# A selective scan in a fused kernel: chunk 0's work goes first on every engine, and the rest of the layer norm waits until inside the scan

## What is computed

```python
x = x + 0.5 * _L0_ffn_ref(_layernorm(x, axis=-1), ...)   # 64 experts, top 3
x = x + _L0_attn_ref(_layernorm(x, axis=-1), ...)        # selective scan
x = x + 0.5 * _L0_ffn_ref(_layernorm(x, axis=-1), ...)   # the experts again
```

```python
raw, gate = jnp.split(x @ W_in, 2, axis=-1)
h = jax.nn.silu(conv4(raw) + conv_b)
ts, Bmat, C = jnp.split(h @ W_x, [DTR, DTR + DST], axis=-1)
dt = jax.nn.softplus(ts @ W_dt + b_dt)
dA = jnp.exp(dt[..., None] * A)                          # 256 channels x 16 states
dBu = dt[..., None] * Bmat[:, :, None, :] * h[..., None]
y = _ssm(dA, dBu, C) + h * D                             # state = dA*state + dBu; y = <state, C>
return (y * jax.nn.silu(gate)) @ W_out
```

## Time and profile before

| | |
|---|---|
| three runs | 796.94, 797.6, 801.3 us; median 797.6 us |
| the profiled execution | 802.77 us, of which its span 801.0 us |
| busy in the span | PE 667.8 us (83%), DVE 596.5 (74%), POOL 489.8 (61%), ACT 445.5 (56%) |
| granted TensorE clock, mean | 0.934 of full |
| the first expert layer | until about 221 us, with its sums from 185.66 us |
| the scan | first scan at 232.97 us, last one ends at about 589.6 us |
| the second expert layer | from about 597 us to the end |

### The profile page before, as it was taken

How to read it: one execution, slowest core, us unless ns; L and a number is a source line. 1 busy time by engine, 2 the same in 40 slices (tenths; PEclk the granted TensorE clock), 3 DMA queues, 4 the chain that set the end, 5 groups by cost and what they waited for, 6 DMA issues and landing times. The chain is left out here.

```text
span 801.0 us, 27792 instructions
## 1 busy us (share of the span) xinstructions
PE 667.8 (83%) x11782; PEld 399.5 (50%) x11782; DVE 596.5 (74%) x1014; ACT 445.5 (56%) x925; POOL 489.8 (61%) x308
## 2 busy tenths in 40 slices
PE   7537999997957989899999989888988179998957
PEld 3524555566734445454544545454546045554547
DVE  7983444443799999999999999989998944344425
...
GB/s 279 393 321 219 333 322 286 245 56 319 75 140 108 110 108 53 127 96 136 107 123 122 70 135 54 126 108 56 4 37 402 194 19 321 325 323 246 114 122 313
DMA packets 87109, 141.07 MB, mean 176 GB/s; under 512 B 9491, under 2 KB 34717, under 8 KB 85712
## 3 DMA queue, kind: packets, MB, share of 16 engines
...
...
## 5 line engine op out<-in xcount | busy, mean ns | idle before, releaser
L1380 POOL TENSOR_TENSOR BIG<-BIG,R 128x1024 f32<-128x1024 f32 x127 | 305.4, 2435 | 13.6 <-DVE BIG L1301 12.3
L1301 DVE TENSOR_TENSOR_SCAN BIG<-BIG,ps 128x1024 f32<-128x1024 f32 x128 | 285.5, 2269 | 13.5 <-PE ps L925 10.2
L925 PE MATMUL ps<-BIG,stack 64*32 64x128 f32 x8192 | 154.1, 278 | 33.2 <-DVE BIG L1301 28.7
L925 PEld LDWEIGHTS ps<-BIG,stack 64*32 64x32 f32 x8192 | 117.4, 107 | 110.9 <-DVE BIG L1301 80.8
L767 POOL DMA_INDIRECT R<-xn_dram,tok_idx x64 | 65.1, 1018 | 89.7 <-DVE row_idx L700 70.7
L781 POOL DMA_INDIRECT y_dram<-BIG,row_idx x64 | 64.6, 1010 | 84.4 <-DVE BIG L724 38.8
L1170 ACT ACTIVATE BIG<-R,An 128x510 f32<-128x510 f32 x128 | 84.3, 710 | 7.1 <-DVE BIG L1301 7.0
L724 DVE COPY BIG<-ps 128x128 f32<-128x128 f32 x64 | 18.4, 288 | 89.3 <-remote 56.8
L1170 ACT ACTIVATE BIG<-BIG,An 128x510 f32<-128x510 f32 x128 | 83.7, 708 | 0.2
L415 ACT ACTIVATE BIG<-BIG 128x512 f32<-128x512 f32 x64 | 40.2, 628 | 74.4 <-DVE BIG L716 58.1
L409 ACT ACTIVATE BIG<-ps 128x128 f32<-128x128 f32 x64 | 16.9, 265 | 111.5 <-PE ps L533 74.7
...
## 6 DMA issues: line engine op xcount, KB each, us to landing
...
```

What stands on the lines that cost most here:

```text
L925: last = nc.tensor.matmul(ps[CW * slot:CW * slot + CW, 2 * (st % 2) + b, :] .rearrange("p (g k s) -> p k g s", g=2, k=4)[:, k], dT[q % 2][ ...
L1301: nc.vector.tensor_tensor_scan(state[st % 3], dA[:, st % 6].rearrange("p b g t -> p (b g t)"), ps[:, u:u + 2, :].rearrange("p b n -> p (b ...
L1380: nc.gpsimd.tensor_tensor(prod[st % RP], state[st % 3].rearrange("p (b g t) -> p b g t", b=2, g=2), Cf[q % 2][:, 2 * gp:2 * gp + 2].rearra ...
```

## The change

Nothing of the arithmetic's amount in the scan changes; work and waits change places, and the inverse root is computed another way.

- Layer norm: the last 12 tiles' statistics move from ahead of scan 0 to behind scans 9, 10 and 12 of chunk 0. `inverse_root` (13 instructions for 24 tiles) becomes one instruction to open, a logarithm and an exponential on ACT, and four to close (`log_root_closed`), once for 12 tiles ahead of scan 0 and once for the other 12, opened behind scan 13 and closed in chunk 1 behind its scan 3.
- Buffers: `state`, `prod` and `dB` get other columns of BIG, and the decays other slots (`DECAY_SLOT`), so that waits for all eight groups of sums become waits for four, six or none.
- PE: `dbu(0)` goes ahead of `dt_proj(1, ...)`, and `dtu_transposes(0, 1)` ahead of `x_proj(1)`. `gates(0, ...)` and `dtu_transposes(1, 0)` go from behind `dbu(3)` to behind `dbu(4)`.
- ACT: `normalise(1)` goes behind the two `raw_copy(0, ...)`, the two `dtu_copy(0, ...)` ahead of `silu_of(1)`, `decays(0)` ahead of `x_parts(1)`, `decays(2)` ahead of `softplus_rest(1, 1)`, and `gate_copy(0, ...)` from behind `decays(5)` to behind `decays(6)`.
- DVE: two taps of chunk 1 go between `dt(0, 0)` and `dt(0, 1)`; `dt(1, n)` goes one scan later. POOL: `dtu(1, ...)` goes two steps later, and `diagonal(0, 3)` no longer waits for the sums.

```diff
@@ -93,3 +93,3 @@
 STAT_TOTALS = dict(stats=NI, meanvar=NI, rstd=6, root=1)
-NEWTON = 13
+DECAY_SLOT = (0, 4, 1, 5, 2, 3)
 LN_TOTALS = dict(normed=24, normed_act=8, transposed=8, xT=8)
@@ -210,5 +210,6 @@
         dA = BIG[:, 0:6144].rearrange("p (u b g t) -> p u b g t", u=6, b=2, g=2)
-        state = [BIG[:, 6144 + 1024 * u:7168 + 1024 * u] for u in range(3)]
-        prod = [BIG[:, 9216 + 1024 * u:10240 + 1024 * u].rearrange("p (b g t) -> p b g t", b=2, g=2) for u in range(RP)]
-        dB = [BIG[:, 16384 + 4096 * u:20480 + 4096 * u].rearrange("p (k n s) -> p k n s", k=4, n=NS) for u in range(2)]
+        state = [BIG[:, c:c + 1024] for c in (8192, 6144, 7168)]
+        prod = [BIG[:, c:c + 1024].rearrange("p (b g t) -> p b g t", b=2, g=2)
+                for c in (9216, 10240, 11264, 16384, 17408, 18432, 19456)]
+        dB = [BIG[:, c:c + 4096].rearrange("p (k n s) -> p k n s", k=4, n=NS) for c in (12288, 20480)]
         HH = [BIG[:, 24576 + 1024 * u:25600 + 1024 * u].rearrange("p (h t) -> p h t", h=C2) for u in range(3)]
@@ -240,20 +241,26 @@
 
-        def inverse_root(e, S, i0, i1, n):
...
-            step(nc.vector.tensor_scalar(v, mv[:, i0:i1, 1], EPS, None, ALU.add))
-            step(nc.vector.tensor_single_scalar(z.bitcast(I32), v.bitcast(I32), 1, ALU.arith_shift_right))
-            step(nc.vector.tensor_scalar(r.bitcast(I32), z.bitcast(I32), -1.0, float(0x5F3759DF), ALU.mult, ALU.add))
-            for k in range(3):
...
+        def log_root_opened(S, i0, i1):
+            nc.vector.tensor_scalar(rs[:, 0, i0:i1], mv[:, i0:i1, 1], EPS, None, ALU.add).then_inc(S("rstd"), 1)
+        def log_root_scalar(e, S, i0, i1, n, m):
+
+            e.wait_ge(*S.at("rstd", n + 1))
+            nc.scalar.activation(rs[:, 2, i0:i1], rs[:, 0, i0:i1], ACT.Ln).then_inc(S("root"), 1)
+            e.wait_ge(*S.at("root", m + 1))
+            nc.scalar.activation(rs[:, 2, i0:i1], rs[:, 2, i0:i1], ACT.Exp, scale=-0.5).then_inc(S("root"), 1)
+
+        def log_root_closed(e, S, i0, i1, n, m):
...
+            e.wait_ge(*S.at("root", m + 2))
+            nc.vector.tensor_tensor(y, z, z, ALU.mult).then_inc(S("rstd"), 1)
...
@@ -807,4 +814,4 @@
                     wait(e, "prod", STEPS * (b - 1))
-                    if b == 0:
-                        e.wait_ge(*F[0].at("sum", 8))
+                    if b < 2:
+                        e.wait_ge(*F[0].at("sum", 4 + 4 * b))
                     for slot in range(SLOTS):
@@ -913,4 +920,4 @@
                 wait(e, "scanned", st - 1)
-                if st == 0:
-                    e.wait_ge(*F[0].at("x", 8))
+                if st < 2:
+                    e.wait_ge(*F[0].at("x", 6 + 2 * st))
                 if n == 0:
@@ -999,9 +1006,9 @@
             gate_sums(e, F[0], 0, 7)
-            x_proj(1)
             dtu_transposes(0, 1)
+            x_proj(1)
+            dbu(0)
             dt_proj(1, 0)
             dt_proj(1, 1)
-            b_transposes(1)
-            dbu(0)
             dbu(1)
+            b_transposes(1)
             for q in range(NQ + 1):
@@ -1019,7 +1026,8 @@
                             sum_states(q - 1, 1, 1, 1)
-                        if q == 0:
-                            gates(0, 0)
-                            gates(0, 1)
-                        if back:
+                        if q and back:
                             dtu_transposes(b, 0)
+                    if n == 2 and q == 0:
+                        gates(0, 0)
+                        gates(0, 1)
+                        dtu_transposes(1, 0)
                     if n == 2 and front:
@@ -1071,4 +1079,3 @@
                 wait(e, "t_psum", q)
-                if q < 3:
-                    wait(e, "rstd", (6, 12, 12 + NEWTON)[q])
+                wait(e, "rstd", (6, 12, 17, 17, 17, 22, 22, 22)[q])
                 for j in range(4):
@@ -1164,8 +1171,6 @@
                 wait(e, "scanned", st - 5)
-                if st == 0:
-                    e.wait_ge(*F[0].at("sum", 8))
-                    e.wait_ge(*F[0].at("x", 8))
-                    wait(e, "pads", 4)
+                if st < 6:
+                    wait(e, "pads", 5 + 2 * (st // 2))
                 for g in range(2):
-                    last = nc.scalar.activation(dA[:, st % 6, :, g, 1:SEQ], dtR[h][:, j, :].rearrange("p (b t) -> p b t", b=2)[:, :, 1:SEQ], ACT.Exp,
+                    last = nc.scalar.activation(dA[:, DECAY_SLOT[st % 6], :, g, 1:SEQ], dtR[h][:, j, :].rearrange("p (b t) -> p b t", b=2)[:, :, 1:SEQ], ACT.Exp,
                                                 scale=An4[:, cg, 2 * gp + g:2 * gp + g + 1])
@@ -1179,5 +1184,5 @@
             xt_copy(0)
-            normalise(1)
             raw_copy(0, 0)
             raw_copy(0, 1)
+            normalise(1)
             xt_copy(1)
@@ -1191,13 +1196,14 @@
             raw_copy(1, 1)
-            silu_of(1)
-            nc.scalar.preload_act_table_set("natural_log_exp_and_others")
+            log_root_scalar(e, MST, 8, 20, 12, 2)
             dtu_copy(0, 0)
-            x_parts(1)
             dtu_copy(0, 1)
+            silu_of(1)
+            nc.scalar.preload_act_table_set("natural_log_exp_and_others")
             decays(0)
+            x_parts(1)
             decays(1)
             softplus_rest(1, 0)
+            decays(2)
             softplus_rest(1, 1)
             bt_copy(1)
-            decays(2)
             decays(3)
@@ -1210,3 +1216,3 @@
                         decays(STEPS * q + n + 4)
-                    if q == 0 and n == 1:
+                    if q == 0 and n == 2:
                         gate_copy(0, 0)
@@ -1232,2 +1238,4 @@
                         silus(q, f, run, front)
+                    if q == 0 and n == 14:
+                        log_root_scalar(e, MST, 20, NI, 17, 4)
                     if n == 11 and front:
@@ -1257,5 +1265,6 @@
 
-            def statistics(i0, i1, n):
-                wait(e, "meanvar", i1)
-                inverse_root(e, MST, i0, i1, n)
+            def first_steps(*slots):
+                for u in slots:
+                    nc.vector.memset(dA[:, u, :, :, 0:1].rearrange("p b g t -> p (b g) t"), 0.0)\
+                        .then_inc(M("pads"), 1)
 
@@ -1300,3 +1309,3 @@
                 u = 2 * (st % 2)
-                nc.vector.tensor_tensor_scan(state[st % 3], dA[:, st % 6].rearrange("p b g t -> p (b g t)"),
+                nc.vector.tensor_tensor_scan(state[st % 3], dA[:, DECAY_SLOT[st % 6]].rearrange("p b g t -> p (b g t)"),
                                              ps[:, u:u + 2, :].rearrange("p b n -> p (b n)"), 0.0, ALU.mult, ALU.add)\
@@ -1322,2 +1331,3 @@
             root_vector(e, MST, 4, 8, 6, 1)
+            first_steps(*DECAY_SLOT[0:2])
             moe_sum(e, F[0], 2)
@@ -1326,7 +1336,12 @@
             moe_sum(e, F[0], 3)
+            first_steps(*DECAY_SLOT[2:4])
             moe_sum(e, F[0], 4)
             stats(8, 20)
+            wait(e, "meanvar", 20)
+            log_root_opened(MST, 8, 20)
             dt(0, 0)
+            for m in range(2):
+                tap(1, m // 3, m % 3)
             dt(0, 1)
-            for m in range(6):
+            for m in range(2, 6):
                 tap(1, m // 3, m % 3)
@@ -1334,9 +1349,7 @@
                 moe_sum(e, F[0], g)
-            e.wait_ge(*F[0].at("x", 8))
-            nc.vector.memset(dA[:, :, :, :, 0:1].rearrange("p u b g t -> p (u b g) t"), 0.0).then_inc(M("pads"), 1)
+            first_steps(*DECAY_SLOT[4:6])
             diagonal(0, 0)
             diagonal(0, 1)
-            stats(20, NI)
-            statistics(8, NI, 12)
-            wait(e, "pads", 4)
+            log_root_closed(e, MST, 8, 20, 12, 2)
+            wait(e, "pads", 9)
             for q in range(NQ + 1):
@@ -1347,4 +1360,12 @@
                         scan(STEPS * q + n)
-                    if q == 0 and n < C2:
-                        dt(1, n)
+                    if q == 0 and n in (1, 2):
+                        dt(1, n - 1)
+                    if q == 0 and n in (9, 10, 12):
+                        i0 = 20 + 4 * (9, 10, 12).index(n)
+                        stats(i0, i0 + 4)
+                    if q == 0 and n == 13:
+                        wait(e, "meanvar", NI)
+                        log_root_opened(MST, 20, NI)
+                    if q == 1 and n == 3:
+                        log_root_closed(e, MST, 20, NI, 17, 4)
                     if q >= 1 and n == 0 and back:
@@ -1400,7 +1421,7 @@
                 for n in range(STEPS):
-                    if n < C2 and q + 1 >= 0 and q + 1 < NQ:
-                        dtu(q + 1, n)
+                    n0 = 2 if q == 0 else 0
+                    if n0 <= n < n0 + C2 and 0 <= q + 1 < NQ:
+                        dtu(q + 1, n - n0)
                     if n == 9 and q + 1 >= 0 and q + 1 < NQ:
                         if q == -1:
-                            e.wait_ge(*F[0].at("sum", 8))
                             diagonal(0, 3)
```

29 lines of the change are left out of this document (14 added, 15 removed).

## The result

The changed kernel takes 807.92 us in the median of four runs (803.87 to 809.6). The kernel before, run beside it, takes 797.63 (796.94 to 801.3). The ratio is 1.0102, with a 95% interval of 1.0057 to 1.0146: slower by 1.0%. The median lies beyond the range on record, whose upper end was 803.5.

What follows compares the result with a forecast made beforehand. It took DVE's scans to bound the kernel, with ACT and PE deciding scan 0. +0.7 us at full clock plus 2.0 for PE's lower clock gave +2.7 on the median of 797.6: 800.3 us, range 794.5 to 803.5.

Steps and rivals of the forecast that it cites:

- In chunk 1 DVE closes the root for 0.8 us: Chunk 1, ahead of where DVE waits for PE: closing the root costs 0.8 us, with nothing to hide it.
- the sum: Whole kernel: +0.7 us with PE at full clock plus 2.0 for the lower clock, +2.7 us.
- the way in: Up to scan 0: DVE ready 7.7 us earlier, but ACT and PE decide; scan 0 at 227.5, 5.5 us earlier.
- forecast for full clock: Chunks 0 and 1, PE at full clock: lead 5.5 us at scan 0, 0.1 at scan 16; cost +0.7 us.
- the clock: Chunk 0: after 4.6 us idle PE runs at 1.2 GHz from `dtu_transposes(1, 0)` to raw(2, 0), losing 2.0 us.
- (b): PE's clock low from 224 on and for 6 us from 244.1: +5.1 us, 802.7; chance 0.22.
- (a): Chunk 0's lead of 4.9 us at scan 4 survives: chance 0.15 for -4 and beyond, 0.15 for -1 to -4.
- my own case: The change does what it says at scan 0 and nothing more than the sum: -1 to +4 us, chance 0.45.
- (c): ACT's table loads each add a drain of about 1.38 us: +5.5 us, 803.1; chance 0.03.

Runs made afterwards that it cites:

- r1: The changed kernel run again unaltered, on another chip: 791.17 us, ratio 1.0107 to the kernel before.
- r3: The changed kernel with idle matmuls on PE, twelve ahead of `x_proj(1)` and nineteen ahead of `dtu_transposes(1, 0)`: 791.52 us, ratio 1.0122 to the kernel before.
- r12: The changed kernel with the same idle matmuls on PE ahead of `x_proj(1)` and `dtu_transposes(1, 0)`, run once more: 812.74 us, ratio 1.0156 to the kernel before.
- r9: The changed kernel with the root's second closing on POOL, between its products of chunk 1's fourth and fifth steps: 802.66 us, ratio 1.0031 to the kernel before.
- r6: The kernel before plus four unused small DVE instructions, one SBUF input and a constant, behind scan 3 of chunks 1 to 7: 833.15 us, ratio 1.0368.
- r2: The changed kernel with the last 12 statistics and their root's opening and closing back ahead of scan 0: 783.76 us, ratio 1.0011 to the kernel before.

## Why the prediction was wrong

**The step that failed** is "In chunk 1 DVE closes the root for 0.8 us". Its four instructions were put at 0.2 us each, from rows in which POOL ran nothing. Beside POOL's products the pauses of 0.92 and 2.28 us come, and from scan 19 to scan 20 it is 3.6 us longer than before, in every profile with small instructions at this place. What follows was not in the prediction at all: PE waits 3.19 us for the late scan, in r1, r3 and r12 its clock falls behind that, and the scans lose another 1.1 to 1.3 us. In all chunk 1 is 3.7 us (result) to 5.1 us (r12: 50.5 for 45.4) longer. r9 takes away that closing alone and chunk 1 is 45.6. The pauses alone carry the sum from +2.7 to +5.5, which is 803.1 and still just inside the range; with r12's 5.1 it is +7.0.

The rows for it stood there. The earlier trace rows has the diagonals at 2.27 and 2.92 us beside POOL. The 1.23 of the earlier trace rows, taken as the duration when POOL makes no diagonal, isn't one with POOL idle: POOL was at its products then, and it was one of them that waited. POOL's timeline before:

```profile
240.70 8.00 POOL L1380 TENSOR_TENSOR BIG<-BIG,R 128x1024 f32<-128x1024 f32 x3
```

Three products take 8.00 us where they take 7.01 elsewhere. So either of the two can be the one that waits. The prediction allowed for POOL with the large instructions and not with the small ones.

The Trainium skill ("SBUF — State Buffer", section "Who interferes with whom") states the rule that I should have weighed: VectorE with two SBUF inputs, or in a mode that uses both ports, and GpSimd take a shared pair of ports for a whole instruction, and the second blocks fully until the first is done. The trace agrees, with DVE's 2.28 us ending 0.03 us behind the end of the product. It also fits r6, since the Trainium skill ("VectorE: DVE Perf Modes", section "Mode 2×_2P — use both read ports for one tensor") counts a float32 `tensor_scalar` from SBUF among the instructions that use both.

**Right: the way in.** DVE is ready 3.7 us behind the eighth sum (forecast 4.2), ACT and PE decide scan 0, and the gate copies end at 248.25, 23.4 behind it (forecast 23.0). DVE's wait ahead of scan 5 was 2.56 us (forecast about 2; the profile names no releaser, but `dbu(5)` ended just ahead of it). With the clock kept, r3 and r12 meet the forecast for full clock at each step: scan 0 at 6.7 (6.4), scan 1 at 10.4 (10.3), scan 4 at 19.7 (19.4), scan 5 at 25.3 (25.3), scan 7 at 32.0 (32.2), scan 16 at 58.8 (59.3).

**Too small: the clock.** I put it at 2.0 us. Against r3 and r12 the changed kernel loses 1.3 to 1.4 us at scan 0, 2.3 at scan 5, 3.2 to 4.3 at scan 16, and 2.9 to 3.0 at scan 32. The part ahead of scan 0, which I had left to rival (b), did come. From the gate copies to scan 5 it was 4.1 us instead of 2.3, as the PE rows at 248.40 show.

**The sum, as measured up to scan 32:** -0.6 at scan 16 with full clock (58.8 for 59.4; forecast -0.1), +2.9 for the clock (2.0), +5.1 for the closing (0.8; in the 5.1, which is r12's, the lower clock behind the closing has some 1.1): +7.4, which is 112.2 against 104.8. The forecast was 2.7. The timed ratios of 1.0102 and 1.0107 are 8.1 and 8.4 us. From scan 32 to scan 127 the changed kernel takes 259.8 us and the one before 261.4, so nothing more was lost there; where the last 1 us of the timed difference lies isn't shown.

**Rivals.** (a) did not come: the lead of 3.9 at scan 0 is 1.0 at scan 5 and gone by scan 7. (b) named the clock rightly at both places. For scan 16 it had +4.3 and my own case +1.9, and the measured +2.6 (r1) and +3.7 (result) lie between the two; it had the same 0.8 for the closing. (c) is refuted here: the gap behind each table load is 0.02 us or less, where the Trainium skill ("ScalarE: Activation LUTs", section "What ACT_TABLE_LOAD costs") adds a drain of about 1.38 us. The time was near (c)'s by another mechanism.

**Where the change's own gain went.** DVE is ready for scan 0 8.1 us sooner (3.7 us behind the eighth sum for 11.8), but 4.3 us of that are a wait for PE, and the work that had filled them was paid for later at a worse price: 1.7 us in chunk 0 and, with the clock behind it, 4.8 in chunk 1 (r1 against r2).
